# Second attention in a six-stage fused vision tower: its two PSUM banks laid out anew, with the four order lists

## The chip, the cores and the metric

The kernel runs on one core of one Trainium2 chip. The core has a matrix engine (PE, TensorE), a vector engine (DVE), a scalar engine (ACT), GpSimd (POOL) and a queue for transfers (SP). PE writes to eight banks of an accumulator memory (PSUM), which DVE and ACT read; POOL does not read it here. The metric is the device time in microseconds of one execution.

## The reference, cut to what matters

128 images of 3x64x64 pixels are cut into 16 patches each and pass through one tower: patch embedding, a class token in front (17 tokens of width 192), attention with a top-k mask, a gated feed-forward layer with quantised weights, a second, causal and linear attention with a gate of its own, and a last feed-forward layer. What the change touches is the second attention:

```python
x_norm = _ln(x, ln_w, ln_b)
qkv = x_norm @ Wqkv + bqkv
q, k, v = jnp.split(qkv, 3, axis=-1)
params = (jax.nn.silu(x @ Wb1) @ Wb2).reshape(B, L, H, 5)
...
interference = jnp.tanh(sem_amp * ctx_amp * jnp.cos(sem_phase - ctx_phase)) * temp
gate = jax.nn.sigmoid(interference)
q_f = (jax.nn.elu(q) + 1.0).reshape(B, L, H, d)
k_f = (jax.nn.elu(k) + 1.0).reshape(B, L, H, d)
kv_gated = jnp.einsum('blhd,blhe->blhde', k_f, v_f) * (1.0 + gate)[..., None, None]
kv_states = jnp.cumsum(kv_gated, axis=1)
z_states = jnp.cumsum(k_f, axis=1)
out_num = jnp.einsum('blhd,blhde->blhe', q_f, kv_states)
```

## The kernel before, in words

Seven images (119 rows of tokens) are a group, and there are 19 groups. The work on a group is cut into six stages, and in step `i` of a software pipeline of 24 steps stage `n` works on group `i - n`. Steps 0 to 6 and the last few are written out; the rest run in a loop of two steps each. Every engine has a list of its own (lines 573, 901, 1069 and 1433) of pairs (stage, work), and goes through it once in each step, in that order; a piece whose stage has no group in this step is left out. An engine never passes over a piece that waits: what stands behind it waits too. Nothing but these lists and the semaphores sets the order.

Stage 0 cuts strips of pixels into patches (POOL, line 491), turns and embeds them, normalises and makes v of the first attention. Stage 1 makes q and k, the scores and the top-k mask; stage 2 the softmax, its product with v and the projection, and at its end the statistics for the feed-forward layer; stage 3 that layer and the norms for the second attention; stage 4 the second attention; stage 5 the last feed-forward layer and the store.

The second attention of a group passes from stage 3 to stage 4. Its pieces by name:

- `v_norms2` (DVE) normalises the rows twice, `t_norms2` (PE) turns them with four transposes, `a_norms_T` (ACT) copies them out of PSUM.
- `t_lin_in` (PE) makes v and the hidden layer of the gate (`hid`), and then q and k with eight matmuls at line 1345.
- `a_tanh_hid`, `v_hidT`, `t_params`, `a_tanh_par` (the gate's parameters), `p_gate` on POOL (a chain of some twenty small instructions up to `overlap`), `a_interference` (two tanh) and `v_v1` (the gated v, DVE line 839) follow one another.
- `a_qk1`, `v_feat` and `p_feat_k` make the features of q and k; `t_lin` multiplies them (heads 0 and 1 of three first, then the third), `v_causal` masks them, `t_num` multiplies them with v, and needs `v_v1`.
- `v_ratio`, `p_centred_sq`, `p_rstd_h`, `v_att1`, `t_att1`, `t_proj1`, `v_h3` end the stage; `v_stats3`, `p_rstd3`, `v_norm3` (DVE line 875) and `t_norm3` lead to stage 5.

All of this has two PSUM banks, `L0` and `L1`. Before the change the turned norms, v, the gate's hidden layer, its parameters, one of the three masked products, the numerators and the projection are in `L0`; q and k, the other two products and the turned `att1` are in `L1`. So `t_norms2` of the next group may not write `L0` until `v_h3` has read the projection: `after(pe, S["h3"], g)`.

## Time and profile before

| | us |
|---|---|
| median of 3 runs | 689.39 (688.89 to 694.93) |
| the profiled execution | 690.81 |
| its span in the trace | 689.0 |
| PE busy | 590.4 (86% of the span) |
| DVE busy | 526.8 (76%) |
| POOL busy | 353.7 (51%) |
| ACT busy | 257.3 (37%) |

The span is the time from the first to the last instruction in the trace; the execution takes 1.8 us more. In the middle of the span PE and DVE are busy in nine tenths and more; at its end, from about 590 us on, fewer stages have a group, all engines are busy less, and the granted clock of PE falls. A row of a timeline gives the start, the duration, the engine, the line, the operation, what it writes and reads, and how many instructions are merged. Starts of successive instructions of one engine can be closer than their durations, since they overlap in the engine.

### The profile page before, as it was taken

The page shows a single profiled execution, that of the slowest core. Times are in us where ns is not written, and L with a number is a line of the kernel's source. Part 1 is how long each engine was busy: PE and PEld are TensorE (multiplying, and loading weights), DVE is VectorE, ACT ScalarE, POOL GpSimd, SP SyncE. Part 2 cuts the span into 40 slices and gives each one's busy share as a digit, 9 for nine tenths or more (in the row PEclk, how much of TensorE's full clock was granted, in tenths as well). Part 3 has the DMA queues.
Part 4 walks back from the last instruction along what each step waited for, and adds up shares of the span by engine and source line. Part 5 has one row for each costly group of instructions (what it writes and reads, how often), then busy time and mean ns, then how long its engine had stood idle before and what let it go on. Part 6 is the DMA issues. An engine that isn't in the chain of part 4 may idle for free.

```text
span 689.0 us, 15353 instructions
## 1 busy us (share of the span) xinstructions
PE 590.4 (86%) x5065; PEld 482.3 (70%) x5065; DVE 526.8 (76%) x2149; ACT 257.3 (37%) x659; POOL 353.7 (51%) x884
## 2 busy tenths in 40 slices
PE   4367888999999999999999999999999998868562
PEld 3165667877878787787878778787877877756451
DVE  0527458798898989889898988989898898774432
ACT  2014233443535344353534435353444534233110
POOL 2001023666656666565666657566665746464432
PEclk9969999999999999999999999999999999685555
DMA  9620010000000000000000000000000000000000
GB/s 218 146 74 0 2 42 21 2 21 7 21 8 21 27 8 21 7 20 5 22 24 5 20 5 20 9 22 20 5 0 5 1 7 8 0 7 1 5 1 7
DMA packets 11122, 14.92 MB, mean 22 GB/s; under 512 B 2161, under 2 KB 8658, under 8 KB 11078
## 3 DMA queue, kind: packets, MB, share of 16 engines
q1 hardware_dynamic: 8774, 12.69, 7.4%
q10 hardware_dynamic: 2304, 1.67, 0.9%
q8 instruction: 24, 0.39, 0.2%
q14 instruction: 20, 0.16, 0.1%
HBM read 12.68 MB, written 1.67 MB: 21 GB/s over the span
## 4 chain that ended last, share of the span: by engine, by line
PE 57%; DVE 21%; POOL 6%; issue 6%; SPq 4%; ACT 4%; DMA 1%; DVEq 0%; POOLq 0%
PE bank_embed L1210 8%; PE bank_lin L1367 6%; PE bank_embed L1215 5%; PE bank_att L1086 4%; PE bank_embed L1180 4%; DVE kept L718 4%; PE bank_att L1274 3%; PE bank_att L1284 3%; SPq L387 3%; PE bank_lin L1086 3%; POOL rstd_h L483 3%; DVE norm L875 2%; PE bank_lin L1383 2%; PE bank_ffn L1426 2%; PE bank_lin L1345 2%
## 5 line engine op out<-in xcount | busy, mean ns | idle before, releaser
L1210 PE MATMUL bank_embed<-norm0T,w_qkv 128*128 128x119 f32 x456 | 63.3, 291 | 8.6 <-DMA g_out<-L_ffn_g_out 6.9
L482 POOL TENSOR_TENSOR spread<-moments,gain_eps 119x1 f32<-119x1 f32 x57 | 12.1, 213 | 113.6 <-DVE moments L673 113.0
L1210 PEld LDWEIGHTS bank_embed<-norm0T,w_qkv 128*128 128x128 f32 x456 | 57.2, 201 | 11.1 <-issue 6.9
L483 POOL TENSOR_TENSOR rstd<-spread,minus_half 119x1 f32<-119x1 f32 (+1 forms) x95 | 55.6, 585 | 7.5
L698 DVE TENSOR_REDUCE scores<-bank_att 119x51 f32<-119x357 f32 x76 | 39.4, 522 | 14.5 <-PE bank_att L1244 13.3
L530 POOL TENSOR_TENSOR feat_k<-feat_qk,consts 96x238 f32<-96x238 f32 x38 | 23.2, 627 | 47.6 <-DVE feat_qk L833 47.6
L1367 PE MATMUL bank_lin<-feat_qk,feat_k 32*119 32x119 f32 x456 | 45.7, 295 | 0.9 <-issue 0.8
L1367 PEld LDWEIGHTS bank_lin<-feat_qk,feat_k 32*119 32x119 f32 x456 | 38.3, 197 | 11.2 <-issue 9.1
L483 POOL TENSOR_TENSOR rstd_h<-spread_h,minus_half 119x12 f32<-119x12 f32 x19 | 43.3, 2277 | 1.5
L1180 PE MATMUL bank_embed<-w_tok,patchT 128*119 128x192 f32 x228 | 42.8, 340 | 0.6 <-ACT patchT L959 0.6
L983 ACT COPY qkT<-bank_embed 128x357 f32<-128x357 f32 x76 | 31.1, 465 | 28.9 <-PE bank_embed L1215 28.9
L742 DVE TENSOR_TENSOR weightsT<-bank_lin,consts 119x476 f32<-119x476 f32 x57 | 36.5, 643 | 6.8 <-PE bank_lin L1367 6.7
L949 ACT COPY probsT<-bank_att 119x476 f32<-119x476 f32 x57 | 31.6, 554 | 25.8 <-PE bank_att L1086 24.4
L1284 PE MATMUL bank_att<-w_o,att0T 128*119 128x192 f32 x228 | 40.2, 326 | 0.0
L553 POOL TENSOR_TENSOR centred_sq<-centred 119x192 f32<-119x192 f32 x19 | 11.5, 603 | 55.0 <-DVE centred L851 55.0
L949 ACT COPY att1T<-bank_lin 96x238 f32<-96x238 f32 x19 | 6.7, 353 | 87.6 <-PE bank_lin L1086 87.6
L1345 PE MATMUL bank_lin<-norms2T,w_qkv 97*96 97x119 f32 (+1 forms) x304 | 39.0, 286 | 0.0
L1180 PEld LDWEIGHTS bank_embed<-w_tok,patchT 128*119 128x119 f32 x228 | 38.1, 190 | 1.1 <-ACT patchT L959 0.8
L1215 PE MATMUL bank_embed<-norm0T,w_qkv_rest 64*128 64x119 f32 x456 | 37.3, 299 | 0.0
L1345 PEld LDWEIGHTS bank_lin<-norms2T,w_qkv 97*96 97x96 f32 (+1 forms) x304 | 37.0, 182 | 0.0
L1284 PEld LDWEIGHTS bank_att<-w_o,att0T 128*119 128x119 f32 x228 | 36.4, 183 | 0.0
L752 DVE TENSOR_TENSOR wide<-probs,consts 119x476 f32<-119x476 f32 x57 | 35.4, 672 | 0.7
(232 smaller groups left out, 1588.2 us busy)
## 6 DMA issues: line engine op xcount, KB each, us to landing
strips<-x SPq DMA_DIRECT2D x19, 336.0 KB
out<-result ACTq DMA_DIRECT2D x18, 89.2 KB
w_qkv<-L_attn_w_qkv SPq DMA_DIRECT2D x2, 576.0 KB, 8.2
w_in_raw<-L_ffn_w_in SPq DMA_DIRECT2D x1, 768.0 KB, 12.6
w_tok_raw<-L_tok_W SPq DMA_DIRECT2D x1, 576.0 KB
w_qkv_rest<-L_attn_w_qkv SPq DMA_DIRECT2D x2, 288.0 KB, 9.9
w_o<-L_attn_w_out SPq DMA_DIRECT2D x1, 576.0 KB
w_qkv_raw<-L_attn_Wqkv SPq DMA_DIRECT2D x1, 432.0 KB
```

Source lines behind the costliest of these rows:

```text
L483: pool.tensor_tensor(rstd_out, spread, minus_half[0:ROWS, 0:spread.shape[1]], ALU.pow) \
L698: dve.tensor_reduce(scores[:, place:place + 3, TOKENS - 1::-1], src[0:ROWS, 0:3 * ROWS].rearrange("p (h b j) -> p h j b", h=3, b=PER), X, ...
L742: dve.tensor_tensor(dst, parts(src, 4)[0:ROWS], mask.unsqueeze(1).to_broadcast([ROWS, 4, ROWS]), ALU.mult).then_inc(ready_sem, 1)
L752: dve.tensor_tensor(wide[:, 4 * f:4 * f + 4], probs[:, 4 * f:4 * f + 4, :].unsqueeze(2).to_broadcast([ROWS, 4, PER, TOKENS]), block_mask.r ...
L949: act.copy(dst, src).then_inc(done_sem, 1)
L1086: return pe.transpose(dst, src, identity)
L1180: last = pe.matmul(E0[0:ROWS, 0:EMBED], patchT[:, k, :], w_tok[:, k, :], start=k == 0, stop=k == CHUNKS - 1)
L1210: pe.matmul(parts((E0, E1)[s], 3)[:, j], w_qkv0[:, tile * 128:(tile + 1) * 128], norm0T[:, s, :], start=j == 0, stop=False, skip_group_che ...
L1215: last = pe.matmul(parts((E0, E1)[s], 3)[:, j], w_qkv0_rest[rows, n, j * 128:(j + 1) * 128], norm0T[rows, 1 - s, :], start=False, stop=j = ...
L1284: last = pe.matmul(A1[0:ROWS, 0:EMBED], att0T[:, t, :], w_o0[:, t, :], start=t == 0, stop=t == QTILES - 1)
L1345: last = pe.matmul(parts(L1, 4)[0:HALF, j], w_qkv1[0:rows, k, j * HALF:(j + 1) * HALF], norms2T[0:rows, 2 + k, :], start=k == 0, stop=k == 1)
L1367: last = pe.matmul(parts((L1, L0, L1)[q], 4)[0:ROWS, 2 * t + odd], feat_k[32 * q:32 * q + 32, odd, t, :], feat_qk[32 * q:32 * q + 32, t, : ...
```

## The change

The two banks are laid out anew. The turned norms go to `L1`, where q and k are made as before; v and the hidden layer of the gate stay in `L0`, and the turned `att1` moves to `L0`. `t_lin_in` is split in two: `t_qk1` (q and k, in `L1`) needs the copied norms alone, and `t_hid` (v and the gate's hidden layer, in `L0`) waits for `v_h3` too. `t_norms2` no longer waits for `v_h3`, but for the mask of the third product (`a_masked2`), which is the last reader of `L1`. `v_norms2` gets a wait for the turn of the norms of the group before. The order lists of all four engines are written anew. No arithmetic is added or taken away.

```diff
             def v_norms2(g, p):
                 dve.wait_ge(S["rstd2"], g + 1)
+                after(dve, S["norms_turned"], g)
...
-            a_norms_T = copy_step([S["norms_turned"]], norms2T[0:HALF, :, :], parts(L0, 4)[0:HALF], S["norms_copied"])
+            a_norms_T = copy_step([S["norms_turned"]], norms2T[0:HALF, :, :], parts(L1, 4)[0:HALF], S["norms_copied"])
...
-            a_att1_T = copy_step([S["att1_turned"]], att1T[0:HALF, :, :], parts(L1, 2)[0:HALF], S["att1_copied"])
+            a_att1_T = copy_step([S["att1_turned"]], att1T[0:HALF, :, :], parts(L0, 2)[0:HALF], S["att1_copied"])
...
             def t_norms2(g, p):
                 pe.wait_ge(S["norms2"], g + 1)
-                after(pe, S["h3"], g)
+                after(pe, S["a_masked2"], g)
                 for n in range(2):
                     for k in range(2):
-                        last = turn(parts(L0, 4)[0:HALF, 2 * n + k], norms2[:, n, k * HALF:(k + 1) * HALF],
+                        last = turn(parts(L1, 4)[0:HALF, 2 * n + k], norms2[:, n, k * HALF:(k + 1) * HALF],
                                     ident[0:ROWS, 0:ROWS])
                 last.then_inc(S["norms_turned"], 1)
 
-            def t_lin_in(g, p):
+            def t_hid(g, p):
                 pe.wait_ge(S["norms_copied"], g + 1)
-
+                after(pe, S["h3"], g)
...
                 last.then_inc(S["hid"], 1)
 
+            def t_qk1(g, p):
+                pe.wait_ge(S["norms_copied"], g + 1)
                 for j in range(4):
...
-                (5, p_rstd3), (0, p_strips), (1, p_h0), (4, p_feat_k), (4, p_gate), (3, p_scaled), (3, p_rms), (5, p_rstd4),
+                (1, p_h0), (0, p_strips), (5, p_h3_beta), (5, p_rstd3), (4, p_feat_k), (4, p_gate), (3, p_scaled), (3, p_rms),
...
-                (0, t_embed), (1, t_dots(1)), (4, t_att1), (4, t_proj1), (0, t_norm0), (3, t_norms2), (0, t_v),
+                (1, t_dots(1)), (4, t_att1), (3, t_norms2), (4, t_proj1), (0, t_norm0), (3, t_qk1), (0, t_v), (3, t_hid),
```

PE, the end of a step and the start of the next, before: the transposes of `att1`, the projection, the first norm, the turned norms of the second attention, v of the first attention (L1194, L1198), v and hidden layer of the second (L1335, L1339), its q and k (L1345), the turned norm of stage 5, the gate's parameters (L1351), q of the first attention.

```order
L1086 MATMUL bank_lin<-consts,att 96x119 x2
L1405 MATMUL bank_lin<-w_p,att1T 119x192 x2
L1086 MATMUL bank_embed<-consts,norm 128x119 x2
L1086 MATMUL bank_lin<-consts,norms 96x119 x4
L1194 MATMUL bank_embed<-w_qkv,norm0T 119x384 x2
L1198 MATMUL bank_embed<-w_qkv_rest,norm0T 119x384 x2
L1335 MATMUL bank_lin<-w_qkv,norms2T 119x192 x2
L1339 MATMUL bank_lin<-norms2T,w_g 128x119 x2
L1345 MATMUL bank_lin<-norms2T,w_qkv 96x119 x8
L1086 MATMUL bank_ffn<-consts,norm 96x119 x2
L1351 MATMUL bank_lin<-w_g,hidT 119x60
L1210 MATMUL bank_embed<-norm0T,w_qkv 128x119 x6
```

The same stretch of PE, now, from behind the transposes of `att1` on (some line numbers differ by one):

```order
L1086 MATMUL bank_lin<-consts,norms 96x119 x4
L1406 MATMUL bank_lin<-w_p,att1T 119x192 x2
L1086 MATMUL bank_embed<-consts,norm 128x119 x2
L1346 MATMUL bank_lin<-norms2T,w_qkv 96x119 x8
L1194 MATMUL bank_embed<-w_qkv,norm0T 119x384 x2
L1198 MATMUL bank_embed<-w_qkv_rest,norm0T 119x384 x2
L1335 MATMUL bank_lin<-w_qkv,norms2T 119x192 x2
L1338 MATMUL bank_lin<-norms2T,w_g 128x119 x2
L1086 MATMUL bank_ffn<-consts,norm 96x119 x2
L1210 MATMUL bank_embed<-norm0T,w_qkv 128x119 x6
L1215 MATMUL bank_embed<-norm0T,w_qkv_rest 128x119 x6
L1352 MATMUL bank_lin<-w_g,hidT 119x60
```

The turned norms stand ahead of the projection instead of behind the first norm, q and k come before v and the hidden layer, and the parameters come behind q of the first attention.

ACT, the middle of a step, before: the copy of the turned int_in, a copy of turned softmax rows (one of three), the gate's tanh of the feed-forward layer, another such copy, the two tanh of the interference, the sum of squares.

```order
L949 COPY int_inT<-bank_ffn 96x238
L949 COPY probsT<-bank_att 119x476
L1009 ACTIVATE tanh_gate<-bank_ffn,unit_in 119x512
L949 COPY probsT<-bank_att 119x476
L1046 ACTIVATE tanh_over<-overlap 119x12
L1048 ACTIVATE tanh_int<-tanh_over,temp 119x12
L1014 ACTIVATE squares,square_sum<-product,half_c 119x512
L949 COPY att0T<-bank_att 128x357
L983 COPY qkT<-bank_embed 128x357 x2
```

ACT, the same stretch, now:

```order
L950 COPY int_inT<-bank_ffn 96x238
L950 COPY probsT<-bank_att 119x476 x2
L1010 ACTIVATE tanh_gate<-bank_ffn,unit_in 119x512
L984 COPY qkT<-bank_embed 128x357 x2
L950 COPY probsT<-bank_att 119x476
L1015 ACTIVATE squares,square_sum<-product,half_c 119x512
L1047 ACTIVATE tanh_over<-overlap 119x12
L1049 ACTIVATE tanh_int<-tanh_over,temp 119x12
L950 COPY numT<-bank_lin 128x357
```

The copies of k of the first attention (`qkT`) and the sum of squares, which stood behind the two tanh, stand ahead of them now.

POOL, where one step ends and the next begins, before (the first row is h3 + beta, then the rstd of stage 5, then the cutting of strips, then h0 plus its bias):

```order
L567 TENSOR_TENSOR h_beta<-h,beta 119x192
L482 TENSOR_TENSOR spread<-moments,gain_eps 119x1
L483 TENSOR_TENSOR rstd<-spread,minus_half 119x1
L490 TENSOR_TENSOR pad_pool<-pad_pool,ones 128x1
L491 COPY patches<-strips 84x1024
L501 TENSOR_TENSOR h<-h,b_o 119x192
```

POOL, the same stretch, now:

```order
L501 TENSOR_TENSOR h<-h,b_o 119x192
L490 TENSOR_TENSOR pad_pool<-pad_pool,ones 128x1
L491 COPY patches<-strips 84x1024
L567 TENSOR_TENSOR h_beta<-h,beta 119x192
L482 TENSOR_TENSOR spread<-moments,gain_eps 119x1
L483 TENSOR_TENSOR rstd<-spread,minus_half 119x1
```

The strips are cut ahead of h3 + beta and of the rstd of stage 5 instead of behind them.

## Rows read from the trace of the kernel before

**Rows 1.** Windows: busy us (instructions) by engine, PE clock, DMA: twelve full steps; tail.
```profile
177.68:536.80 359.12, 339.77 (x3157) 281.93 (x3157) 322.60 (x1334) 157.90 (x408) 223.67 (x540) 1.00 0.05 14
...
595.73:689.00 93.27, 58.98 (x343) 46.45 (x341) 42.79 (x132) 20.51 (x55) 41.17 (x110) 0.57 0.01 4
```

**Rows 2.** Waits of PE in 327 to 357 us: us in total, times, longest.
```profile
PE bank_ffn L1086 <- DVE norm L875: 1.2, 2, 0.7
PE bank_lin L1405 <- ACT att1T L949: 0.4, 1, 0.4
PE bank_lin L1086 <- DVE h L866: 0.3, 1, 0.3
```

**Rows 3.** Waits of DVE in 327 to 357 us.
```profile
DVE v L839 <- ACT tanh_int L1048: 1.1, 1, 1.1
...
DVE row_gain L798 <- POOL rms_inv L483: 0.2, 1, 0.2
```

**Rows 4.** Timeline of PE, one full step: start us, us, engine line op, tiles.
```profile
326.70 0.41 PE L1086 MATMUL bank_ffn<-consts,norm 119*96 119x119 f32 x2 [0.52 <-DVE norm L875]
...
333.99 1.09 PE L1367 MATMUL bank_lin<-feat_qk,feat_k 32*119 32x119 f32 x8
...
337.39 1.46 PE L1274 MATMUL bank_att<-probsT,v 119*64 119x119 f32 x24
...
356.76 0.38 PE L1086 MATMUL bank_ffn<-consts,norm 119*96 119x119 f32 x2 [0.70 <-DVE norm L875]
```

**Rows 5.** Timeline of ACT in the same step.
```profile
329.60 0.82 ACT L983 COPY qkT<-bank_embed 128x357 f32<-128x357 f32 x2 [0.58 <-PE bank_embed L1215]
...
334.25 0.55 ACT L949 COPY probsT<-bank_att 119x476 f32<-119x476 f32 x1
336.88 0.21 ACT L1046 ACTIVATE tanh_over<-overlap 119x12 f32<-119x12 f32 x1 [2.09 <-POOL overlap L549]
...
337.34 0.71 ACT L1014 ACTIVATE squares<-product,half_c 119x512 f32<-119x512 f32 x1
337.95 0.19 ACT L1014 ACTIVATION_READ_ACCUMULATOR squares<-product,half_c 119x1 f32 x1
```

**Rows 6.** Timeline of DVE in the same step.
```profile
337.47 0.85 DVE L839 SCALAR_TENSOR_TENSOR v<-tanh_int,v_raw 119x192 f32<-119x192 f32 x1 [1.11 <-ACT tanh_int L1048]
...
355.55 0.97 DVE L875 TENSOR_SCALAR norm<-h,moments,rstd 119x192 f32<-119x192 f32 x1 [0.17 <-issue]
```

**Rows 7.** Timeline of POOL in the same step.
```profile
336.81 1.29 POOL L517 TENSOR_TENSOR scaled<-product,g_out 119x512 f32<-119x512 f32 x1
...
355.38 1.03 POOL L491 COPY patches<-strips 84x1024 f32<-84x1024 f32 x1
```

**Rows 8.** Line 875, whole run: duration ns min/median/max, first and last start.
```profile
L875 DVE TENSOR_SCALAR norm<-h,moments,rstd x19: 376/1216/1220, 145.9 to 680.4; 119x192 f32<-119x192 f32 x19
```

**Rows 9.** Line 839, the same.
```profile
L839 DVE SCALAR_TENSOR_TENSOR v<-tanh_int,v_raw x19: 359/840/1093, 128.1 to 666.4; 119x192 f32<-119x192 f32 x19
```

**Rows 10.** Timeline of PE in the last step that has a stage 4.
```profile
650.07 1.00 PE L1086 MATMUL bank_lin<-consts,norms 119*96 119x119 f32 x4 [0.54 <-DVE h L866]
651.71 1.63 PE L1335 MATMUL bank_lin<-w_qkv,norms2T 97*119 97x192 f32 x4 [0.64 <-ACT norms2T L949]
...
653.98 3.38 PE L1345 MATMUL bank_lin<-norms2T,w_qkv 97*96 97x119 f32 x16
...
657.55 0.51 PE L1351 MATMUL bank_lin<-w_g,hidT 128*119 128x60 f32 x2
```

**Rows 11.** Timeline of DVE, the same step.
```profile
647.63 0.67 DVE L819 TENSOR_SCALAR norms<-h,moments,rstd 119x192 f32<-119x192 f32 x2 [0.87 <-POOL rstd L483]
...
666.42 0.36 DVE L839 SCALAR_TENSOR_TENSOR v<-tanh_int,v_raw 119x192 f32<-119x192 f32 x1 [0.71 <-ACT tanh_int L1048]
```

**Rows 12.** Timeline of POOL, the same step.
```profile
660.11 0.37 POOL L537 TENSOR_TENSOR amp<-tanh_par,ones 119x12 f32<-119x12 f32 x2
...
666.03 0.56 POOL L483 TENSOR_TENSOR rstd<-spread,minus_half 119x1 f32<-119x1 f32 x1
```

More of the change, by code:

```diff
@@ L1069, in _ @@
             iterations(act, lambda i, parity, active: in_turn(i, parity, active, [
[L1070 to L1075 removed]
+                (4, a_tanh_par), (3, a_int_in), (5, a_hid1), (1, a_qk(0)), (3, a_in_T), (2, a_probsT[1]), (2, a_probsT[0]),
+                (3, a_tanh_gate), (1, a_qk(1)), (2, a_probsT[2]), (3, a_square), (4, a_interference), (4, a_num_T),
+                (2, a_att[0]), (0, a_patchT(0, E0, S["patches0"], S["patchT0"])), (2, a_att[1]), (3, a_int_out), (3, a_out_T),
+                (0, a_patchT(1, E1, S["patches1"], S["patchT1"])), (4, a_att1_T), (3, a_norms_T), (0, a_norm0T), (3, a_qk1),
+                (0, a_v(1)), (0, a_v(0)), (3, a_tanh_hid), (5, a_store), (4, a_norm3_T), (1, a_exp),
             ]), setup)
@@ L1397, in t_att1 @@
                 for k in range(2):
-                    last = turn(parts(L1, 2)[0:HALF, k], flat[:, k * HALF:(k + 1) * HALF], ident[0:ROWS, 0:ROWS])
+                    last = turn(parts(L0, 2)[0:HALF, k], flat[:, k * HALF:(k + 1) * HALF], ident[0:ROWS, 0:ROWS])
                 last.then_inc(S["att1_turned"], 1)
```

26 lines of the change are left out of this document (10 added, 16 removed).

## The prediction

> **What bounds the kernel now.** I read the page first (which engines are busy, and that the chain that ended last runs mostly over PE and DVE), then windows over full steps and over the tail, then the waits of PE and DVE inside one step, and last the timelines of that step, engine by engine. In twelve full steps PE is busy 339.77 of 359.12 us and DVE 322.60 [rows 1]; one step takes 359.12/12 = 29.93 us. PE waits in a step for the turned `att1`, 0.4 us, for h3, 0.3, and for the norm of stage 5, 1.2 in two steps, 0.6 each [rows 2]: some 1.3 us in all, and no layout can give back more than that per full step, since the matmuls stay. DVE has only a little more idle time: 1.1 us for the gate's tanh, 0.2 for `rms_inv` [rows 3], and small gaps. So two engines are nearly full, and a step is a ring: DVE ends the norm of stage 5, PE turns it and goes on, the gate's tanh come out on ACT, DVE makes the gated v and works on without a long wait up to the next norm. What counts is how long one turn of this ring takes. In the tail it is otherwise: PE is busy 58.98 of 93.27 us and its granted clock is 0.57 on average, that is mostly the lower level of 1.2 GHz [rows 1]. There the latency of the second attention sets the pace.
>
> **The ring in full steps, from the norm's turn on PE to the gated v on DVE.** Before, the turn starts at 326.70 and the softmax product behind k of the first attention at 337.39 [rows 4]: 10.69 us of unbroken PE work. The gated v starts at 337.47 [rows 6], 10.77 after the turn. In the new order the third product (1.09 us in its row, 1.02 without the overlap [rows 4]) and four of the transposes of the softmax (half as many matmuls, so about 0.5) stand behind k and not ahead of it; the parameters only change sides with q. So k is ready at 10.69 - 1.02 - 0.5 = 9.2, plus 0.1 for the last matmul: 9.3. Then ACT must do, in order, what used to stand behind the tanh: the copies of k (0.82), the turned softmax (0.55), the squares (0.71, and 0.19 for reading their sum) and the two tanh, from 336.88 to the start of v at 337.47, that is 0.59 [rows 5, 6]. With 0.1 of overlap at each of the first two hand-overs, and again before the sum is read, this is 0.82 + 0.55 + 0.71 + 0.19 + 0.59 - 0.3 = 2.56. The gated v starts at 9.3 + 2.6 = **11.9 after the turn instead of 10.77: 1.1 us later**. The chain of the gate on POOL is not what it waits for: overlap is there before tanh_over's old start at 336.88, 10.2 after the turn, and the parameters move by no more than 0.1 against it, since feat_k no longer stands in the way. The third product ends at 9.3 + 0.5 + 1.0 = 10.8 and its mask 0.6 later, 11.4, also in time.
>
> **The ring from the gated v to the next turn.** Before, 356.76 - 337.47 = 19.29 us [rows 4, 6]. Four things come off.
> - The norm of stage 5. It takes 1.216 us in the median, and 0.376 at its shortest [rows 8]; at 355.55 it takes 0.97 and ends just behind the copy of the strips on POOL, which runs from 355.38 for 1.03 [rows 6, 7]. The two go together. In the new order the strips are cut ahead of h3 + beta, in the time when DVE makes the top-k, and the norm meets no large POOL instruction. That is 1.22 - 0.38 = 0.84 in one of two steps and 0.97 - 0.38 = 0.59 in the other: **0.7**.
> - The gated v. It takes 0.840 in the median and 0.359 at its shortest [rows 9], and at 337.47 lies beside POOL's scaled, 336.81 to 338.10 [rows 6, 7]. Scaled does not wait for v and starts as before some 10.1 after the turn, so it ends at 11.4, half a microsecond ahead of the new v: **0.5**.
> - The wait of 0.2 for `rms_inv` [rows 3]: the squares now come before the tanh, so the sum is there earlier: **0.2**.
> - Nothing else: the waits of PE for the turned `att1` and h3 go, but they are not on the ring. Their place is taken by a wait for `norms2`, which now is wanted right behind the transposes of `att1`, at the same 0.4 or so. PE has the slack for it, since it waits for the norm of stage 5 in any case.
>
> The Trainium skill, page "SBUF — State Buffer", section "Who interferes with whom", says that a DVE instruction with two SBUF inputs, or in a two-port mode, and a GpSimd instruction lock each other out for the whole of the one that came first. For the strips and for scaled the trace agrees. Taken to the letter it speaks against the change, as v now falls on the power instruction of `rms_inv` or of the next rstd. The trace does not bear that out: in the tail v at 666.42 takes its shortest time, 0.36, in the middle of POOL's rstd, 666.03 to 666.59 [rows 11, 12]. I cost it at nothing, and at 0.5 us as a bound.
>
> Sum of a full step: 1.1 - 0.7 - 0.5 - 0.2 = -0.3. The step that I took is 30.06 long, 0.1 above the mean, and a DVE wait for the embedding may go too (small gaps); I take **-0.4 per step**, 29.5 us. The ends are -1.3, if all of PE's waits go and PE alone bounds, and +1.1, if neither lengthened instruction gets shorter. There are 14 steps with all six stages: 14 x -0.4 = **-5.6 us**. The steps of the fill (four) have fewer stages and the same orders; I put them at 0, within 1.5 either way.
>
> **The tail.** In the last step with a stage 4 the norms were ready at 647.63 + 0.67 = 648.30 [rows 11] and waited for h3 until 650.07; v and the hidden layer started at 651.71, q and k, 3.38 us at the lower clock, at 653.98, and only then the parameters, at 657.55 [rows 10]; POOL could begin the gate at 660.11, behind feat_k, and v came at 666.42 [rows 11, 12]. Now the norms are turned before the projection, which starts about 649.3, 1.4 later than it could, and takes 1.4; q and k issue until 650.75 + 3.2 = 653.9, v and the hidden layer until 656.2. The tanh, its product and the handovers need 1.0: parameters at 657.2. But feat_k is long done, so the gate starts some 0.8 behind that, at 658.0 and not at 660.11: **-2** for this step. In the two steps before, the feed-forward layer's matmuls and the masks stand between, which only move by what q and k no longer hold back: **-1 each**. Sum -4, with 0 and -6 as ends. What follows the last h3 is unchanged. The waits added (`norms_turned` on DVE, `a_masked2` on PE) are for things done some ten microseconds before; nothing queues behind them.
>
> **Sum.** -5.6 - 4 = -9.6 us against the profiled execution of 690.81, of which the median of the runs is 689.39, 1.4 lower. From the median: 689.4 - 9.6 = 679.8, **680 us**.
>
> **The rivals.**
> - *Only the tail gains.* If ACT or PE needs 0.4 more to the tanh (a copy that waits for PE, an issue gap), full steps stay at 29.9: 689.4 - 4 = 685.4. For it: the ring's saving is small against the many handovers in it, and DVE gets two waits it did not have (for out4 and for the third product). Against it: both have over half a microsecond of slack by the sum above.
> - *PE bounds alone.* If the handovers are tighter than I count, the full steps fall by 0.8: 689.4 - 11 - 4 = 674. For it: PE is free of h3 and `att1`; against it: it still waits for two DVE results.
> - *Slower: the gated v stays on the ring, late and long.* If the gate's chain on POOL slips by 0.5, scaled slips with it and runs into v. v then keeps its 0.84, and ACT's order makes it late by 1.1 all the same. If moreover the norm is not freed, the step is longer by 1.1 - 0.2 = 0.9: 689.4 + 12.6 - 4 = 698. The point from which this decides is 0.4 us lost per step, that is v starting later than 12.3 after the turn. For it: v's start hangs on six ACT instructions in a row; against it: the strips are plainly moved.
> - *The lock to the letter.* v waits 0.5 for POOL's power instruction in each step: the full steps stay at 29.5 + 0.5 = 30.0, and the time is 689.4 + 1 - 4 = 686. The page is the one on SBUF of the Trainium skill named above.
>
> **How the numbers follow.** Forecast 0.54 (its own range 676.5 to 684); only the tail 0.18; lock to the letter 0.08; PE alone 0.13; slower 0.07. About 1% (6.9 us) is what a measurement of this kernel can tell from no change. Faster by over 1% is below 682.5: most of the forecast (0.46) and PE alone, 0.59. Slower by over 1%, above 696.3: 0.06. Within: 0.35. The range of 8 in 10 runs from 673.5, the case of PE alone, to 688.5, beyond the case of the tail and of the lock; what is left out is the slower case and the edges of the others.
>
> **What would show it.** The norm of stage 5 at 0.38 and the gated v at about 0.36 us in full steps; the strips beside the top-k; the tanh_over about 11.3 us behind the norm's turn; no wait of PE for h3, a new one for `norms2` of about 0.4; a step of 29.5 us; in the tail v some 2 us earlier against the transposes of `att1` ahead of it. It would be wrong if the norm stayed at 0.9 us and more, if v started over 12.3 us behind the turn, or if another DVE instruction grew beside the moved strips.

## The result: 4% faster, well beyond the forecast

| | us | runs |
|---|---|---|
| before | 692.16 (688.89 to 697.18) | 4 |
| changed kernel | 664.7 (663.96 to 665.34) | 4 |
| ratio | 0.9597 (0.9527 to 0.9667) | |

An execution that takes over 1.5% longer than the fastest of its kernel is left out of the medians here and below (one was, of hid_first_filled2).

The sign was right and the size was not: 680 was forecast, from 673.5 to 688.5, and the time lies below that range. The span fell from 689.0 to 662.9 us. To see where the 26.1 us come from, I cut both spans at the starts of stage 5's norm (L875 before, L876 now), which comes once per group: the first of the 19, the 14th and the last. Between the first and the 14th lie 13 of the 14 steps with all six stages. The 14th of them is the first interval of the next column: it runs from the 14th norm to the 15th and takes 30.18 us before and 28.78 now.

| | first norm at | 13 full steps | one of them | 14th to 19th norm | rest |
|---|---|---|---|---|---|
| before | 145.93 | 389.00 | 29.92 | 145.43 | 8.6 |
| changed | 142.17 | 376.71 | 28.98 | 135.43 | 8.6 |
| difference | -3.8 | -12.3 | -0.94 | -10.0 | 0.0 |

The fill's 3.8 us can't be put down to the change. Over all traces of this case the first norm starts between 143.3 and 147.7 with the old order lists, and between 141.1 and 154.2 with the new ones. So the 14 full steps gave 12.3 + 1.4 = 13.7 us where 5.6 were forecast, and what comes behind them, from the 15th norm to the last, gave 8.6 where 4 were.

The windows of the full steps and of the tail, the changed kernel (us of the stretch, then PE, PEld, DVE, ACT and POOL busy, granted clock, DMA share, GB/s):

```profile
142.17:518.88 376.71, 367.78 (x3422) 304.41 (x3420) 329.53 (x1445) 168.70 (x442) 240.73 (x585) 1.00 0.05 14
518.88:662.90 144.02, 104.38 (x839) 85.59 (x838) 92.77 (x358) 44.38 (x118) 75.01 (x193) 0.78 0.02 5
```

The same two stretches before:

```profile
145.93:534.93 389.00, 368.12 (x3422) 305.43 (x3421) 349.53 (x1445) 171.06 (x442) 242.26 (x586) 1.00 0.05 14
534.93:689.00 154.07, 114.03 (x845) 92.90 (x843) 96.54 (x358) 44.94 (x118) 76.32 (x196) 0.72 0.02 4
```

In full steps PE's work is the same to 0.4 us (367.78 against 368.12), and what it stands idle fell from 20.9 to 8.9 us. DVE works 20.0 us less (329.53 against 349.53), with as many instructions: some of them have become shorter. In the tail PE has the same number of instructions to within six and is busy 9.6 us less, at a mean clock of 0.78 and not 0.72.

**The full step.** Its rows in the changed kernel answer to [rows 2] to [rows 9]. First PE's timeline (start us, us, engine, line, tiles, count):

```profile
316.42 0.41 PE L1086 MATMUL bank_ffn<-consts,norm 119*96 119x119 f32 x2 [0.20 <-DVE norm L876]
...
325.33 0.68 PE L1086 MATMUL bank_att<-consts,wide 119*119 119x119 f32 x4
...
345.63 0.41 PE L1086 MATMUL bank_ffn<-consts,norm 119*96 119x119 f32 x2 [0.63 <-DVE norm L876]
```

ACT, the chain to the gated v:

```profile
325.44 0.81 ACT L984 COPY qkT<-bank_embed 128x357 f32<-128x357 f32 x2 [1.46 <-PE bank_embed L1215]
326.14 0.57 ACT L950 COPY probsT<-bank_att 119x476 f32<-119x476 f32 x1
326.59 0.74 ACT L1015 ACTIVATE squares<-product,half_c 119x512 f32<-119x512 f32 x1
...
327.31 0.22 ACT L1047 ACTIVATE tanh_over<-overlap 119x12 f32<-119x12 f32 x1
327.56 0.30 ACT L1049 ACTIVATE tanh_int<-tanh_over,temp 119x12 f32<-119x12 f32 x1
```

DVE, the norm of stage 5, the mask of the third product and the gated v:

```profile
315.99 0.37 DVE L876 TENSOR_SCALAR norm<-h,moments,rstd 119x192 f32<-119x192 f32 x1
...
327.06 0.65 DVE L742 TENSOR_TENSOR weightsT<-bank_lin,consts 119x476 f32<-119x476 f32 x1 [1.04 <-PE bank_lin L1368]
327.90 0.36 DVE L840 SCALAR_TENSOR_TENSOR v<-tanh_int,v_raw 119x192 f32<-119x192 f32 x1 [0.19 <-ACT tanh_int L1049]
```

POOL, the cutting of strips, now ahead of everything of stage 5, and scaled:

```profile
311.76 1.03 POOL L491 COPY patches<-strips 84x1024 f32<-84x1024 f32 x1
...
326.46 1.29 POOL L517 TENSOR_TENSOR scaled<-product,g_out 119x512 f32<-119x512 f32 x1
```

ACT starts the last copy of k at 325.44, 9.02 behind the turn at 316.42, and from there to the gated v at 327.90 it is 2.46: together 11.48 us, where the forecast had 9.3, 2.56 and 11.9, and 10.77 was before. scaled ends at 327.75, 11.33 behind the turn (forecast 11.4), and v starts 0.15 later and takes 0.36. The strips end at 312.8, three microseconds ahead of the norm, which takes 0.37. The durations of the two lines over the whole run (ns, min/median/max):

```profile
L876 DVE TENSOR_SCALAR norm<-h,moments,rstd x19: 373/375/380, 142.2 to 654.3; 119x192 f32<-119x192 f32 x19
...
L840 DVE SCALAR_TENSOR_TENSOR v<-tanh_int,v_raw x19: 347/359/618, 125.2 to 640.4; 119x192 f32<-119x192 f32 x19
```

PE's waits over two steps, 316.4 to 374.5 us (total, times, longest):

```profile
PE bank_ffn L1086 <- DVE norm L876: 1.0, 3, 0.6
```

DVE's over the same:

```profile
DVE weightsT L742 <- PE bank_lin L1368: 2.1, 2, 1.0
DVE out L881 <- PE bank_ffn L1432: 1.7, 2, 1.0
DVE v L840 <- ACT tanh_int L1049: 0.4, 2, 0.2
```

PE's waits for the turned `att1` and for h3 [rows 2] are gone, and none for `norms2` came in their place. DVE's wait for the tanh fell from 1.1 in a step [rows 3] to 0.2, and DVE waits instead for PE's third product and for out4, ahead of v, where it had nothing to wait for before.

**The tail.** PE of the changed kernel, in the last step but one that has a stage 4 (the step that answers to [rows 10] comes next):

```profile
599.67 1.03 PE L1086 MATMUL bank_lin<-consts,norms 119*96 119x119 f32 x4 [0.91 <-DVE norms L820]
...
601.77 3.04 PE L1346 MATMUL bank_lin<-norms2T,w_qkv 97*96 97x119 f32 x16
604.65 0.82 PE L1335 MATMUL bank_lin<-w_qkv,norms2T 97*119 97x192 f32 x4
...
606.86 0.42 PE L1352 MATMUL bank_lin<-w_g,hidT 128*119 128x60 f32 x2 [0.75 <-DVE hidT L827]
607.12 0.66 PE L1427 MATMUL bank_ffn<-norm3T,w 97*128 97x119 f32 x4
607.70 1.09 PE L1368 MATMUL bank_lin<-feat_qk,feat_k 32*119 32x119 f32 x16
```

The same step before:

```profile
619.31 1.00 PE L1086 MATMUL bank_lin<-consts,norms 119*96 119x119 f32 x4 [0.54 <-DVE h L866]
620.95 1.63 PE L1335 MATMUL bank_lin<-w_qkv,norms2T 97*119 97x192 f32 x4 [0.64 <-ACT norms2T L949]
...
623.21 3.38 PE L1345 MATMUL bank_lin<-norms2T,w_qkv 97*96 97x119 f32 x16
...
628.19 1.21 PE L1426 MATMUL bank_ffn<-norm3T,w 97*128 97x119 f32 x4 [0.90 <-ACT norm3T L949]
629.48 1.95 PE L1367 MATMUL bank_lin<-feat_qk,feat_k 32*119 32x119 f32 x16
```

The 16 masked products of `t_lin`, its quadrants 0 and 1, take 1.95 us before and 1.09 now, the hidden layer of stage 5 1.21 and 0.66. (A quadrant holds the features of four of the twelve heads; the description of the kernel before calls the three quadrants heads.) These are the same instructions on the same tiles. 1.09 is what the products take in full steps, at a granted clock of 1.00 (2.4 GHz). The granted clock is the third number from the right. Before, from the turned norms to the end of the products:

```profile
619.31:631.43 12.12, 10.50 (x53) 9.45 (x54) 3.11 (x15) 2.93 (x9) 4.14 (x14) 0.50 0.00 0
```

Now, for the turned norms and the projection, for q and k, and from there to the products:

```profile
599.67:601.77 2.10, 2.10 (x8) 2.07 (x9) 0.00 (x0) 0.55 (x1) 0.36 (x1) 0.50 0.00 0
601.77:604.65 2.88, 2.88 (x18) 2.87 (x16) 1.28 (x5) 0.00 (x0) 1.34 (x3) 0.56 0.00 0
604.65:608.79 4.14, 3.39 (x35) 2.92 (x34) 2.21 (x11) 2.49 (x8) 2.24 (x8) 1.00 0.09 26
```

Before, PE stays at its lower level (0.50, 1.2 GHz) throughout, with waits of 0.54, 0.64 and 0.90 us among these matmuls. Now it has no wait from the turned norms to the turned norm of stage 5, and the clock rises to its upper level inside q and k; the wait of 0.75 us behind them does not bring it down again. The forecast had no such term.

### The profile page after: what moved, and what is told of

It is laid out like the page before. It is cut to its first block, busy times and chain, and to the rows that moved or that the text cites. A ratio compares the mean times of both kernels' runs of the same rounds, so it can differ in the third digit from the quotient of the medians.

```text
span 662.9 us, 15406 instructions
## 1 busy us (share of the span) xinstructions
PE 577.5 (87%) x5065; PEld 471.7 (71%) x5065; DVE 501.5 (76%) x2149; ACT 254.9 (38%) x659; POOL 352.9 (53%) x884
## 4 chain that ended last, share of the span: by engine, by line
PE 60%; DVE 23%; issue 4%; SPq 4%; ACT 3%; POOL 3%; DMA 1%; DVEq 0%; POOLq 0%; ACTq 0%
PE bank_embed L1210 8%; PE bank_att L1284 6%; PE bank_lin L1368 5%; PE bank_embed L1180 5%; PE bank_embed L1215 5%; DVE kept L718 5%; PE bank_att L1086 4%; PE bank_att L1274 4%; SPq L387 3%; DVE scores L698 3%; PE bank_lin L1384 3%; DVE top L710 2%; PE bank_att L1244 2%; PE bank_ffn L1086 2%; PE bank_lin L1086 2%
## 5 line engine op out<-in xcount | busy, mean ns | idle before, releaser
L1210 PE MATMUL bank_embed<-norm0T,w_qkv 128*128 128x119 f32 x456 | 59.4, 282 | 8.5 <-DMA g_out<-L_ffn_g_out 6.8
L483 POOL TENSOR_TENSOR rstd<-spread,minus_half 119x1 f32<-119x1 f32 (+1 forms) x95 | 57.3, 603 | 7.5
L698 DVE TENSOR_REDUCE scores<-bank_att 119x51 f32<-119x357 f32 x76 | 37.6, 517 | 12.3 <-PE bank_att L1244 11.0
L1368 PE MATMUL bank_lin<-feat_qk,feat_k 32*119 32x119 f32 x456 | 42.5, 277 | 3.0 <-DVE weightsT L742 2.6
L1368 PEld LDWEIGHTS bank_lin<-feat_qk,feat_k 32*119 32x119 f32 x456 | 35.3, 180 | 7.9 <-DVE weightsT L742 3.4
L950 ACT COPY probsT<-bank_att 119x476 f32<-119x476 f32 x57 | 30.2, 564 | 17.5 <-PE bank_att L1086 17.5
```

What stands on the lines that cost most here:

```text
L483: pool.tensor_tensor(rstd_out, spread, minus_half[0:ROWS, 0:spread.shape[1]], ALU.pow) \
L698: dve.tensor_reduce(scores[:, place:place + 3, TOKENS - 1::-1], src[0:ROWS, 0:3 * ROWS].rearrange("p (h b j) -> p h j b", h=3, b=PER), X, ...
L950: act.copy(dst, src).then_inc(done_sem, 1)
L1210: pe.matmul(parts((E0, E1)[s], 3)[:, j], w_qkv0[:, tile * 128:(tile + 1) * 128], norm0T[:, s, :], start=j == 0, stop=False, skip_group_che ...
L1368: last = pe.matmul(parts((L1, L0, L1)[q], 4)[0:ROWS, 2 * t + odd], feat_k[32 * q:32 * q + 32, odd, t, :], feat_qk[32 * q:32 * q + 32, t, : ...
```

## The experiments

All times are medians, with the ratio to the kernel before run beside it on the same chip. "Step" is the mean of the 13 full steps and "tail" the time from the 14th to the 19th norm (its first interval is still a full step), both of the profiled execution.

| kernel | time | ratio (95%) | step | tail |
|---|---|---|---|---|
| again | 667.07 | 0.966 (0.963 to 0.970) | 28.98 | 132.0 |
| pool_only | 681.62 | 0.985 (0.980 to 0.990) | 29.22 | 146.7 |
| pool_back | 678.27 | 0.981 (0.975 to 0.987) | 29.74 | 135.9 |
| layout_only | 686.79 | 0.996 (0.993 to 0.999) | 29.92 | 143.6 |
| pe_on_ring | 676.46 | 0.977 (0.972 to 0.983) | 29.41 | 134.8 |
| pe_off_ring | 668.61 | 0.967 (0.962 to 0.971) | 28.97 | 134.3 |
| act_on_ring | 677.56 | 0.981 (0.975 to 0.986) | 29.48 | 135.3 |
| tanh_first | 664.48 | 0.962 (0.957 to 0.967) | 28.91 | 133.1 |
| tail_hid_first | 682.13 | 0.989 (0.984 to 0.994) | 28.98 | 147.2 |
| warm_before | 687.60 | 0.994 (0.991 to 0.998) | 29.93 | 144.6 |
| warm_tail | 664.04 | 0.966 (0.959 to 0.973) | 28.97 | 132.8 |
| warm_tanh | 663.70 | 0.961 (0.956 to 0.966) | 28.91 | 132.0 |
| hid_first_filled | 670.41 | 0.971 (0.965 to 0.976) | 28.98 | 138.0 |
| hid_first_filled2 | 668.16 | 0.975 (0.967 to 0.983) | 28.98 | 139.1 |
| before_filled | 684.35 | 0.989 (0.986 to 0.992) | 29.93 | 138.8 |

**again** is the changed kernel with nothing but a comment edited: it says how far two traces of one kernel differ.

```diff
-# ---- launch
+# ---- launch again
```

> The changed kernel once more, for its spread and for a second trace of the fill. 664.7 us within 1. If the 2.4 us that step 1 of the fill lost in the kernel before (33.55 against 35.95 us between the first two embeddings) come from the orders, the gap is 33.5 here too; if they come from the granted clock of that moment, it moves between traces of one kernel.

The median, 667.07, lies outside the microsecond that was allowed (663.28 to 669.4, 6 runs). The step came out at 28.98 again, to a hundredth, and the tail at 132.0, 3.4 less than in the first trace. So a step is known to 0.01 us, and a tail to some 3. Nearly all of the 3.4 lies in one interval, from the 16th norm to the 17th, 27.67 us in the first trace and 24.40 here. In it the 8 products of the third quadrant take 1.95 us at a granted clock of 0.50 in the first trace and 1.09 at 1.00 here: one program, two levels of the clock. The gap between the first two embeddings is 35.94 us before, 33.55 in the first trace of the changed kernel and 32.16 here, so it too moves between traces of one kernel.

### The full step: what gave 0.94 us

**pool_only** puts the new list of POOL into the kernel before; **pool_back** puts the old one into the changed kernel.

```diff
-  (5, p_rstd3), (0, p_strips), (1, p_h0), (4, p_feat_k), ...
+  (1, p_h0), (0, p_strips), (5, p_h3_beta), (5, p_rstd3), (4, p_feat_k), ...
```

> The kernel before with the changed order list of POOL alone: the strips are cut ahead of h3 + beta and of the rstd of stage 5. Ring theory (the norm of stage 5 is on the ring and its copy of the strips beside it costs 0.6 to 0.8): the norm takes 0.38 us, a full step falls from 29.93 to 29.3 (PE waits 0.6 for that norm in each step, and no more than that can go), the time by 14 x 0.6 = 8 to 9 us. Rival (the norm is only one of several things that end together, PE next): the norm takes 0.38, the step stays above 29.7, the time within 3 us of before.

> The changed kernel with POOL's old order list: the strips are cut again behind the rstd of stage 5. Ring theory: the norm grows back to about 1.0 to 1.2 and the step from 29.0 to 29.6 or 29.8, the time from 664.7 to 674 or 676. Rival (another wait takes over, the share of POOL's order is small): below 668.

Forward, the list alone takes the step from 29.92 to 29.22, by 0.70; backward, from 28.98 to 29.74, by 0.76. The norm's line in pool_only and in pool_back, whole run:

```profile
L875 DVE TENSOR_SCALAR norm<-h,moments,rstd x19: 370/375/380, 147.0 to 673.6; 119x192 f32<-119x192 f32 x19
```

```profile
L876 DVE TENSOR_SCALAR norm<-h,moments,rstd x19: 375/1215/1220, 146.9 to 669.4; 119x192 f32<-119x192 f32 x19
```

And one step of pool_back, the norm on DVE and the strips on POOL:

```profile
325.56 1.22 DVE L876 TENSOR_SCALAR norm<-h,moments,rstd 119x192 f32<-119x192 f32 x1
```

```profile
325.63 1.03 POOL L491 COPY patches<-strips 84x1024 f32<-84x1024 f32 x1
```

Both start within 0.1 us, and the norm ends 0.12 behind the strips: with the old list it is as long as POOL's copy leaves it, with the new one 0.38. The list of POOL is worth 0.70 to 0.76 of the step's 0.94. pool_back came out at 678.27 us, 2 above what was expected, with its step inside (29.74).

**layout_only** has the new places of the tiles, the split of `t_lin_in` and the new waits, with the work in the old order.

```diff
-            a_att1_T = copy_step([S["att1_turned"]], att1T[0:HALF, :, :], parts(L1, 2)[0:HALF], S["att1_copied"])
+            a_att1_T = copy_step([S["att1_turned"]], att1T[0:HALF, :, :], parts(L0, 2)[0:HALF], S["att1_copied"])
...
-                after(pe, S["h3"], g)
+                after(pe, S["a_masked2"], g)
...
-                (4, t_lin_in), (5, t_norm3), (4, t_params), ...
+                (4, t_hid), (4, t_qk1), (5, t_norm3), (4, t_params), ...
```

> The new layout of the two PSUM banks and the new waits, with the four order lists of before (t_hid and t_qk1 stand one behind the other where t_lin_in stood). Ring theory: PE's wait for h3 goes (0.33 in a step) but is not on the ring, since PE waits for the norm of stage 5 behind it: the full step stays 29.9; the tail gains 1 to 2 us in each of three steps, since the norms are turned before h3: 686 us. Rival (the layout is what the gain comes from): full steps below 29.6 and a time below 680.

The step stays at 29.92 and the tail gives 1.8. In full steps the new places are worth nothing by themselves: what they do is to permit the order.

**pe_on_ring** issues two of q's first matmuls twice in stage 1, between the turn of the norm and the gated v; **pe_off_ring** issues one more matmul ahead of v of the second attention, between the gated v and the next turn. Their results are written over by the real ones.

```diff
+                            for _ in range(2 if n == 0 and j == 0 else 1):
                                 pe.matmul(parts((E0, E1)[s], 3)[:, j], w_qkv0[:, tile * 128:(tile + 1) * 128], ...
```

```diff
                 after(pe, S["h3"], g)
+                pe.matmul(L0[0:ROWS, 128:128 + EMBED], norms2T[0:HALF, 2, :], w_qkv1[0:HALF, 0, 2 * EMBED:3 * EMBED],
+                          start=True, stop=True)
```

> The changed kernel with PE work added between the turn of stage 5's norm and the gated v: the first two matmuls of q of the first attention are issued twice (0.24 us each, 0.48 in a step). PE is idle 0.69 us in a full step of the changed kernel, so by PE's own load there is room for it. Ring theory: the work is on the ring, the full step grows by 0.4 to 0.5, from 28.98 to 29.4 or 29.5, the time by 7 to 9 us to about 672 to 674. Rival (PE's total load bounds, place does not matter): below 667, the same as with the same work elsewhere.

> The changed kernel with PE work added behind v of the first attention, ahead of PE's wait for stage 5's norm: one more matmul of v of the second attention (0.38 us in a step), overwritten by the real one. Ring theory: PE waits for the norm there anyway, 0.5 us in the mean (0.2 in one of two steps, 0.6 in the other), so the full step grows by 0.1 at most and the time by 0 to 2 us, to 667 at most. Rival (PE's load bounds): +0.38 in a step, 670 us.

**act_on_ring** lets ACT square the product once more, ahead of the two tanh, into a tile that nobody reads.

```diff
+                act.activation(squares_again[:, :], product[:, :], ACT.Square)
```

> The changed kernel with one more ACT instruction behind the squares, ahead of the two tanh: product squared once more into a tile of its own (0.6 us). ACT is busy 45% of a full step. Ring theory: the six ACT instructions from the copies of k to the second tanh are on the ring, the full step grows by 0.5 to 0.6, the time to 672 to 674. Rival (the third masked product on DVE, which ends 0.2 us before the tanh, or PE sets the pace and ACT has room): within 2 us of 665.

By the windows of the 13 full steps, PE's busy time rose by 5.74 us in pe_on_ring, 0.44 per step, and the step by 0.43; PE's idle time stayed at 0.7 per step. In pe_off_ring it rose by 3.20, 0.25 per step and not the 0.38 expected, and the step did not grow (28.97); PE's idle time shrank from 0.69 to 0.43 per step instead:

```profile
154.17:536.50 382.33, 373.52 (x3474) 310.07 (x3472) 329.16 (x1445) 168.84 (x442) 236.09 (x585) 1.00 0.05 13
147.51:524.12 376.61, 370.98 (x3447) 308.70 (x3446) 330.45 (x1444) 168.45 (x442) 241.11 (x585) 1.00 0.05 14
```

0.6 us more of ACT's work on the ring cost 0.50. So it is the ring that sets the step, and not PE's sum of work, though PE stands idle only 0.7 us per step. The times of pe_on_ring and act_on_ring, 676.46 and 677.56, are 2.5 to 3.6 us above the ranges expected; their steps are inside, and their first norms came late, at 154.2 and 149.3 us. DVE's waits in act_on_ring, 300 to 360 us, show the link that was stretched:

```profile
DVE v L841 <- ACT tanh_int L1051: 1.4, 2, 0.7
```

It was 0.4 in two steps and is 1.4: 0.5 more per step, as much as the step grew.

**tanh_first** moves the gate's two tanh ahead of the squares on ACT.

```diff
-  (2, a_probsT[2]), (3, a_square), (4, a_interference),
+  (2, a_probsT[2]), (4, a_interference), (3, a_square),
```

> The changed kernel with the two tanh ahead of the squares on ACT. They can start at 326.7 instead of 327.31 in the step read, but the third mask on DVE ends at 327.71 and stands ahead of the gated v, so v gains 0.2 at most: ring theory says a full step shorter by 0.1 to 0.2, and 662 to 663 us, unless rms_inv, which then comes 0.5 later, is waited for (it was there 0.2 before it was wanted): then no gain, 665. Rival (v beside POOL's scaled again, which ends at 327.75): v starts at 327.75 at the earliest and must wait no more than 0.05; if it locks, v takes 0.8 and the step grows by 0.4, 670 us.

The step fell by 0.07 only, and the time of 664.48 is that of the case without a gain. v no longer waits, but `row_gain` right behind it now waits 0.3 for the reciprocal root, which comes from the squares:

```profile
DVE row_gain L798 <- POOL rms_inv L483: 0.6, 2, 0.3
```

Squares and tanh are both wanted at once, and one of them is late in either order.

### The tail: the order, or the clock

**tail_hid_first** is the changed kernel in which, in the steps without a stage 0 alone, v and the hidden layer stand ahead of q and k again, on PE and on ACT.

```diff
-  (4, t_att1), (3, t_norms2), (4, t_proj1), (0, t_norm0), (3, t_qk1), (0, t_v), (3, t_hid),
+  (4, t_att1), (3, t_norms2), (4, t_proj1), (0, t_norm0),
+  *([(3, t_hid), (3, t_qk1)] if isinstance(i, int) and i >= GROUPS else [(3, t_qk1), (0, t_v), (3, t_hid)]),
```

> The changed kernel, but in the steps without a stage 0 PE makes v and the gate's hidden layer ahead of q and k, and ACT copies them in that order, as in the kernel before. Order theory: q and k stand ahead of the gate's parameters again and feat_k, which needs them, ahead of the gate on POOL; in each of the last two steps the gate starts some 2.5 us later, in the one before some 1: the tail grows by 5 to 6 us, to about 670 us. Rival (the tail gained by the clock alone, which this order does not lower, since PE works on without a gap): within 2 us of 665.

The tail went to 147.2: 12 us more than in the changed kernel's trace, 15 more than in again's, and more than before the change. The time, 682.13, is far above both expectations, 670 and 665: the order alone was reckoned at 5 to 6 us, and the rival was wrong that PE would work on without a gap. PE in the step shown above, of tail_hid_first:

```profile
605.26 1.60 PE L1335 MATMUL bank_lin<-w_qkv,norms2T 97*119 97x192 f32 x4 [0.54 <-DVE h L867]
...
607.49 3.38 PE L1346 MATMUL bank_lin<-norms2T,w_qkv 97*96 97x119 f32 x16
...
612.92 0.65 PE L1352 MATMUL bank_lin<-w_g,hidT 128*119 128x60 f32 x2 [1.65 <-DVE hidT L827]
...
614.46 1.96 PE L1368 MATMUL bank_lin<-feat_qk,feat_k 32*119 32x119 f32 x16
```

Two waits stand in PE's stream, for h3 (0.54) and for the hidden layer's tanh (1.65), and the matmuls shown run at the lower level, 1.96 us for the products. That leaves two readings, since order and gaps changed together. They do so in every trace here that has no filling: in the last two steps with a stage 4 the 16 products take 1.09 us in all seven traces with the changed kernel's order in the tail (and in warm_tail and warm_tanh), and 1.95, once 1.65, in the five with q and k last.

**warm_before** and **warm_tail** had tried the clock by itself and told little: matmuls whose result nobody reads, ahead of the turn of `att1` (in the kernel before and in the changed one), where PE waits for several microseconds, and 20 of them ahead of the last norm of stage 5. **warm_tanh** is warm_tail with tanh_first's order.

```diff
+                        for _ in range(counts[g]):
+                            pe.matmul(E0[:, 0:ROWS], ident_b[:, :], ident_b[:, 0:ROWS], start=True, stop=True)
...
-  (4, t_att1),
+  (4, t_warm({16: 24, 17: 34, 18: 54})), (4, t_att1),
```

> The kernel before with idle time of PE filled in the last four steps alone: 24, 34 and 54 small matmuls into a bank that is free there, ahead of the transposes of att1 in the last three steps that have a stage 4, and 20 ahead of the last norm of stage 5. They compute nothing that is used. If the clock is a large part of what the tail gained (the masked products take 1.95 us in the tail before, 1.09 in the tail of the changed kernel), the clock in the tail rises, the products take 1.09 here too and the tail is 4 to 7 us shorter: 683 to 686 us. If the order alone made the gain, the tail stays at 145 us, within 1.5.

> The changed kernel with the same small matmuls in the last four steps. Clock theory: what is still at the lower level there, the projection (1.49 and 1.64 us), the turned norms, q and k and the last layer (1.21), gets faster, 1 us in each of three steps and 1 at the end: 661 us. Rival (the matmuls come in the way of att1, or the clock does not answer): 665 to 667.

> The changed kernel with the small matmuls in the tail and with the two tanh ahead of the squares (which gave 0.07 us in a full step): if both add, 660 us.

Tails of 144.6, 132.8 and 132.0: no more than 1 to 3 us below their bases, within what two traces of one kernel differ by, and no time as low as expected. The place was wrong: behind it came further waits, for the norms and for h3, and in warm_before the products still took 1.95 us. Only the 20 matmuls ahead of the last norm gave something of their own: the rest behind it takes 7.7, 7.5 and 7.9 us in the three traces, against 8.6 in all others.

**hid_first_filled** keeps tail_hid_first's order and fills just the two short waits with such matmuls; **hid_first_filled2** does so with more of them.

```diff
+  (3, t_warm({17: 9, 18: 9})), (3, t_hid), (3, t_qk1)
...
+  (4, t_warm({16: 16, 17: 16, 18: 16})), (4, t_params),
```

> tail_hid_first with PE's two short waits of the tail filled by matmuls whose result nobody reads (bf16, 119 columns, some 0.1 us each at 1.2 GHz): 9 of them ahead of v and the hidden layer in the last two steps with a stage 3, where PE waited 0.54 us for h3, and 16 ahead of the parameters, where it waited 1.65 us for hidT. The order of the real work stays that of tail_hid_first, whose tail took 147.2 us. Theory that the order itself is the tail's gain: no change, tail 146 to 148, the masked products stay at 1.96 us, time 682. Theory that the lost gain is the clock that PE's gaps kept at 1.2 GHz: the granted clock rises behind the filled stretch, the products of the third part take 1.09 us, and the tail falls by 5 to 10 us to 137 to 142, time 672 to 677.

> As hid_first_filled, with 24 and 22 such matmuls in place of 9 and 16, so that PE has no gap from the projection of h3 to the products even if they run at 2.4 GHz, at the price of up to 1.9 us more work ahead of v and the hidden layer in two steps. Order theory: the tail gets 2 to 4 us longer, 149 to 151. Clock theory: products at 1.09 us in every step of the tail, tail 136 to 142.

The same step of hid_first_filled (the filling is on line 1439):

```profile
606.91 1.11 PE L1439 MATMUL bank_embed<-ident_b 128*128 128x119 bf16 x9
...
610.01 1.80 PE L1346 MATMUL bank_lin<-norms2T,w_qkv 97*96 97x119 f32 x16
...
613.87 0.42 PE L1352 MATMUL bank_lin<-w_g,hidT 128*119 128x60 f32 x2 [1.00 <-DVE hidT L827]
...
614.71 1.09 PE L1368 MATMUL bank_lin<-feat_qk,feat_k 32*119 32x119 f32 x16
```

q and k take 1.80 and not 3.38, the products 1.09 and not 1.96, and the tail 138.0 instead of 147.2. The waits are not all gone (1.00 us for the hidden layer's tanh remains), and the time, 670.41, is below the range expected, while the tail is inside it. With more matmuls the tail is 139.1: the 16 products take 1.09 there too, and the 1.1 us more are less than two traces of one kernel can differ by.

**before_filled** does the same to the kernel before: 9 such matmuls ahead of the turned norms, 9 ahead of v of the second attention, 16 ahead of stage 5's hidden layer, in three steps.

```diff
+  (4, t_warm({16: 9, 17: 9, 18: 9})), (4, t_lin_in), (5, t_norm3), (4, t_params), (1, t_qk(0)), (5, t_warm({15: 16, 16: 16, 17: 16})), (5, t_hid1),
...
+  (3, t_warm({16: 9, 17: 9, 18: 9})), (3, t_norms2),
```

> The kernel before, with three short waits of PE in each of the last three steps with a stage 4 filled by matmuls whose result nobody reads: 9 ahead of the turn of the norms, where PE waited 0.54 us for h3, 9 ahead of the four products of the second attention, where it waited 0.64 us for the copy of norms2, and 16 ahead of the hidden layer of stage 5, where it waited 1.16 us. Order and tables stay as before. If the tail's gain of the changed kernel is mostly the clock that rises when PE's work there has no gap, the products of the third part fall from 1.95 to 1.09 us and the tail from 145.4 to 136 to 140, time 680 to 684 against 689.5. If it is the order of q and k, v and the hidden layer, the tail stays at 144 to 147 and the time at 688 to 691.

```profile
622.00 1.81 PE L1345 MATMUL bank_lin<-norms2T,w_qkv 97*96 97x119 f32 x16
...
626.70 1.09 PE L1367 MATMUL bank_lin<-feat_qk,feat_k 32*119 32x119 f32 x16 [0.58 <-issue]
```

The old order with its gaps filled has a tail of 138.8, 6.6 less than the 145.4 of its base, all of it in the last three intervals, and 684.35 us against 690.95 beside it (0.35 above the range expected). The clock theory stands: filling the waits among the second attention's matmuls raises PE's clock there in either order. Not every short wait matters: the one of 0.75 us in the changed kernel and the one of 1.00 in hid_first_filled come when the clock has already risen, and the products behind them still take 1.09. The Trainium skill, page "TensorE: Matmul & The Clock Gate", section "A second HAM failure mode: psum-queue depth-cycling", tells of another kernel in which short idles of TensorE between groups of matmuls keep its clock going back and forth between the two levels. The tail here agrees in part: with waits of 0.54 and 1.65 us in tail_hid_first the clock does not go back and forth in the step shown but stays at the lower level.

What is left between before_filled (138.8) and the changed kernel (135.4 and 132.0) is 3.4 to 6.8 us. Of it 1.4 is the full step that the tail column holds; the other 2.0 to 5.4 are the order's own share of the tail, if the filling costs nothing.

## Why the prediction fell short

**The ring: right in kind.** Adding work on it and beside it showed that a step's length is the ring's. Most signs came: v later against the turn, the norm at 0.38, v at 0.36, no wait of PE for h3. Two did not: no wait for `norms2` of 0.4, and the first tanh 10.9 behind the turn and not 11.3. The rival that PE's work bounds alone was nearest in its number for full steps (-0.8), but pe_off_ring refutes its mechanism.

**The step that failed, first: the sum of a full step**, "1.1 - 0.7 - 0.5 - 0.2 = -0.3", taken as -0.4. Over the 13 steps, from the start of the norm to v it is 11.96 us in the mean before and 12.00 now, so +0.04, where 1.1 - 0.7 = +0.4 was forecast. From v to the next norm it is 17.97 and 16.98, so -0.99, where -0.5 - 0.2 = -0.7 was forecast.
- v came 0.7 later against the turn in the step read, 0.8 in the mean (10.69 and 11.50), and not 1.1. ACT could start the last copy of k 9.02 behind the turn and not 9.3 (the four transposes that left the stream have 0.68 us in their row, where I took 0.5), and its chain took 2.46 and not 2.56.
- Behind v, the forecast's two items make 0.7 together, and they came (0.49 and 0.23 in the step read). One more went, which the forecast named and gave 0.1 at most: DVE's wait for the embedding, 0.24 in the step before and none now. The three make 0.96 of the 0.99.
- Of what was counted, the strips were sized right: 0.7 forecast, 0.70 and 0.76 measured by the two POOL runs. So the other lists are worth 0.2 per step. They make v later, which costs, and free it from scaled, which pays for it.

The number of full steps, 14, was right. The range did not follow from the forecast's own ends: -1.3 in each of 14 steps and -6 in the tail give 689.4 - 18.2 - 6 = 665, close to what came, but 673.5 was worked out with -0.8 per step.

**The step that failed, second: the tail at "-2" and "-1 each"**, with 0 and -6 as ends. All its terms were taken from rows at the lower level of the clock, as [rows 10] show it, and were moved about as if that level were given. The moves came: in the tail the time from h3 to v fell from 18.8, 18.7 and 16.9 us to 15.0, 12.1 and 12.8, and from v to h3 it rose by 1.0, 3.1 and 1.4 (in again by 1.0, 1.1 and 1.4). The projection starts late behind the norms, for which 1.4 was forecast. But the clock is an outcome of the order: q and k now cover the time in which h3 is made, and PE has no gap from the turned norms to the turned norm of stage 5. The first row of the forecast had said it, a clock of 0.57 beside PE busy 58.98 of 93.27 us [rows 1], and it was read as a fact of the tail and not as a price of its gaps. By before_filled and the two filled kernels the clock is worth 6.6 to 9.2 us; the order's own 2.0 to 5.4 hold the forecast's 4. So the step that failed is the term that is not there, a change of the clock, which the forecast put at nothing.

**The chances.** The rule of the Trainium skill weighed in the forecast, page "SBUF — State Buffer", section "Who interferes with whom", was that the lock holds for the whole of an instruction. For the strips, these runs show it: a norm of 1.22 beside a copy of 1.03, 0.38 without. Its rival, that v would wait 0.5 for POOL's power instruction, got a chance of 0.08 and didn't come: v's median is 0.36. In some full steps v starts 0.13 us behind the start of POOL's power instruction, inside it, and takes its 0.36 all the same; in others it starts 0.08 ahead, and the power instruction takes 0.69 instead of 0.55. A step of the first kind, and the power instruction behind the v at 327.90:

```profile
357.02 0.55 POOL L483 TENSOR_TENSOR rms_inv<-mean_square,minus_half 119x1 f32<-119x1 f32 x1
357.15 0.36 DVE L840 SCALAR_TENSOR_TENSOR v<-tanh_int,v_raw 119x192 f32<-119x192 f32 x1 [0.19 <-ACT tanh_int L1049]
```

```profile
327.98 0.69 POOL L483 TENSOR_TENSOR rms_inv<-mean_square,minus_half 119x1 f32<-119x1 f32 x1
```

The slower rival needed v 12.3 after the turn; it was 11.48.

**Open.** The tail differs by 3.4 us between two traces of the same kernel, and each filled kernel has one trace, so the split between clock and order is known to no better than that. The 0.2 us per step of the lists of ACT, PE and DVE were not taken apart further. No kernel clearly beats the changed one: warm_tanh, the best, has 663.70 us (660.46 to 668.6, 4 runs), against 664.04 to 667.07 for the kernels nearest to it.

## What to carry to other kernels

Find the ring that sets the step, and try it by adding known work on it and beside it: here 0.44 us more of PE's time on it cost 0.43, and 0.25 beside it nothing, though PE was idle for 0.7 us only. Where the granted clock is low in a stretch, look for short waits between the matmuls there before you price anything by its rows; the same 16 products cost 1.95 or 1.09 us, and filling waits of 0.5 to 1.2 us with matmuls that nobody reads gave 6.6 us to a kernel whose order was left alone. A large copy on POOL belongs where DVE does nothing short and urgent: its place was worth 0.7 us of a 30 us step.

## What of the hardware was not expected

Here the lower clock was not left by added work alone, wherever it was put. 24 to 54 matmuls ahead of the turn of `att1` didn't lift the products from 1.95 us in warm_before; 9, 9 and 16 in the shorter waits nearer to them did so in before_filled, in two of the three filled steps (in the first, PE still waited 0.81 us for the copy of the turned norm, and the products took 1.96). The last 8 products of a step, the third quadrant's, were back at the lower level (1.95 us) in before_filled and hid_first_filled in the last two of these steps, and between the levels (1.32 and 1.52) in hid_first_filled2.

The fill differs as much between traces as between kernels: with the new lists the first norm came anywhere from 141.1 to 154.2 us, with the old ones from 143.3 to 147.7. I did not look for the cause with a run of its own.

In pool_back the norm starts 0.07 us ahead of the strips by the trace, and yet it is the norm that is held, to 0.12 behind the copy's end, while the copy keeps its 1.03. A smaller instruction of POOL (`pad_pool`, 0.21 us from 325.47) runs when the norm starts, so the trace does not say which of the two came first.
